# Deformable convolution of a four-stage network: a third offset buffer, a ring of three tents, and a rearranged start and end

## The chip, the core and the metric

The kernel runs on one core of one Trainium2 chip. Its engines work side by side and meet through semaphores: TensorE (PE, matmuls), VectorE (DVE), ScalarE (ACT), GpSimd (POOL) and SyncE (SP); the last two issue most of the DMAs. The metric is the device time of the core in microseconds, as a median of several runs.

## What is computed

The input is x of 8 images, 16 channels and 64 x 64 pixels, all in float32. Four stages follow one another: a gated scan over both axes (L0), an inverted-bottleneck convolution with mixed experts (L1), two deformable convolutions (L2), and two "distance" convolutions (L3). The change lies in L2, of which this is the core:

```python
def deform_conv(x, w, b, ow, ob):
    off = conv2d(x, ow, ob).reshape(Bn, K, 2, Hh, Ww)
    cy = iy + dy + off[:, :, 0]
    cx = ix + dx + off[:, :, 1]
    y0, x0 = jnp.floor(cy), jnp.floor(cx)
    wy, wx = cy - y0, cx - x0
    samp = gather(y0i, x0i, (1 - wy) * (1 - wx)) + gather(y0i, x0i + 1, (1 - wy) * wx) \
         + gather(y0i + 1, x0i, wy * (1 - wx)) + gather(y0i + 1, x0i + 1, wy * wx)
    return jnp.einsum('bckhw,ock->bohw', samp, w.reshape(w.shape[0], Cin, K)) + b

h = relu(group_norm1(deform_conv(x, w1, b1, ow1, ob1), g1, be1)) + x
h = relu(group_norm1(deform_conv(h, w2, b2, ow2, ob2), g2, be2)) + h
```

For each of K = 9 taps a convolution gives two offsets, the input is sampled bilinearly there, and the samples are contracted with the weights. A group norm over each image follows.

## The kernel before

The program is written engine by engine in one order that never changes: each engine runs its list and waits for semaphores. The two deformable layers are the loop over `L` (0 and 1).

**Offsets.** TensorE computes the offsets of 64 rows in four chunks of 16 rows (`convolve(m)`, L1269, 288 matmuls each). ScalarE copies a chunk out of PSUM (`copy_offsets`, L1049), VectorE bounds it (`bound_offsets`, L704 and L706) and takes the largest magnitude of each row (`reach`, L711; at the last chunk also L716). SyncE stores it to DRAM (`store_offsets`, L449). The raw offsets stand in two halves of `YA`, the bounded ones in two buffers at `D1`. A second rearrangement, DRAM to DRAM, makes one contiguous record of every batch of four rows (`arrange_batch`, L466, also SyncE). Between these TensorE turns the image (`turn_columns`, L1281), and GpSimd stores the turned columns (`store_columns`, L1457).

**Batches.** A layer has `NB` = 16 batches of four image rows, and a batch `NU` = 3 units of column blocks. For batch n GpSimd loads its record, spread over the partitions, in four DMAs of 576 KB (`load_batch`, L1484). It may do so when the record is arranged and the buffer is free: there are two buffers of offsets, so load n waits until the tent products of batch n-2 are ready. ScalarE takes the distances (`distances`, L1056), and for each unit two y terms (`y_terms`, L1067 and L1068). VectorE finishes the x tent of a batch (L723) and multiplies three tents for every unit (L729, L730, L731; nine operations a batch). The products go into a ring of `RING` = 4 slots. TensorE samples with them (`sample`, L1302 and L1307 at the image's edge, 48 or more matmuls a unit), and ScalarE copies the samples from PSUM (`copy_samples`, L1078). ScalarE then writes the y terms for the unit that is `RING` further on. After unit 0 of every second batch TensorE contracts the 18 sampled pieces of the eight rows before (`contract`, L1325 and L1330, 72 matmuls); ScalarE copies the result (`copy_rows`, L1093), and VectorE adds the rows that two contractions share (`add_shared_rows`, L750).

**Windows.** The image columns that a batch samples come from DRAM in four chunks of about 16 rows into two buffers (`load_windows`, L1471, GpSimd), and VectorE spreads the rows of a batch into a ring (`spread_windows`, L416), after unit 0 of the batch.

**Start.** All four offset convolutions precede the first sample on TensorE. ScalarE copies the fourth chunk between the y terms of units 2 and 3, and VectorE bounds it after batch 0.

**End.** When all rows are copied, VectorE counts the taps that reach beyond the bounded window (`far_samples`, from L860), whose table SyncE fetches once batch 14's tents are ready. For these inputs the count is zero and the branch over `far_block` is taken. Then come the statistics of the group norm (`channel_stats`, L534, eight chunks) and the normalisation.

## Time and profile before

| what | us |
|---|---|
| median of 3 runs (911.18 to 913.99) | 912.49 |
| the profiled execution, whole | 907.34 |
| its span in the profile | 905.5 |
| layer 0: tents of batch 0 finished, of batch 15 finished | 302.8, 498.5 |
| layer 1: tents of batch 0 finished, of batch 15 finished | 590.5, 785.4 |
| busy in the span: PE, DVE, ACT, POOL | 652.5, 592.2, 462.5, 124.3 |

All times inside the kernel are counted from the start of the span. The span is that of the core's instructions; the whole execution is 1.8 us longer. The two deformable layers take from about 241 to 814 us, so nearly two thirds of the kernel. A line such as "POOL arena L1484 <- DVE arena L731" says that an engine's instruction of line 1484 stood until one of line 731 on another engine had finished; `arena` is the one large on-chip buffer, and nearly every tile lies in it.

### The profile page before, as it was taken

The page shows a single profiled execution, that of the slowest core. Times are in us where ns is not written, and L with a number is a line of the kernel's source. Part 1 is how long each engine was busy: PE and PEld are TensorE (multiplying, and loading weights), DVE is VectorE, ACT ScalarE, POOL GpSimd, SP SyncE. Part 2 cuts the span into 40 slices and gives each one's busy share as a digit, 9 for nine tenths or more (in the row PEclk, how much of TensorE's full clock was granted, in tenths as well). Part 3 has the DMA queues.
Part 4 walks back from the last instruction along what each step waited for, and adds up shares of the span by engine and source line. Part 5 has one row for each costly group of instructions (what it writes and reads, how often), then busy time and mean ns, then how long its engine had stood idle before and what let it go on. Part 6 is the DMA issues. An engine that isn't in the chain of part 4 may idle for free.

```text
span 905.5 us, 30232 instructions
## 1 busy us (share of the span) xinstructions
PE 652.5 (72%) x13944; PEld 452.1 (50%) x13944; DVE 592.2 (65%) x823; ACT 462.5 (51%) x623; POOL 124.3 (14%) x187
## 2 busy tenths in 40 slices
PE   2409999999987486877787388567776876809493
PEld 1104555567854365655565255346655655605252
DVE  6894062211336978888887444798888888577365
ACT  3505424432332767768776141577777668532423
POOL 6000000000033113122210004222122111000000
PEclk9758999999999889898899779979999898958796
DMA  4000000000058866476543008956667555000002
GB/s 155 0 0 2 2 3 3 3 16 4 17 156 264 292 221 205 182 250 206 183 173 127 1 3 200 344 191 226 240 225 233 174 185 205 10 2 3 1 4 94
DMA packets 27754, 108.73 MB, mean 120 GB/s; under 512 B 10100, under 2 KB 14836, under 8 KB 23528
## 3 DMA queue, kind: packets, MB, share of 16 engines
q0 software_dynamic: 13376, 86.80, 28.5%
q1 hardware_dynamic: 14248, 19.97, 6.9%
q8 instruction: 110, 1.80, 0.8%
q14 instruction: 20, 0.16, 0.1%
HBM read 91.84 MB, written 19.65 MB: 123 GB/s over the span
## 4 chain that ended last, share of the span: by engine, by line
DVE 30%; PE 28%; DMA 21%; ACT 8%; issue 7%; POOL 3%; SPq 2%; DVEq 0%; ACTq 0%; POOLq 0%
DMA arena<-offsets_by_batch 17%; PE psum L1222 13%; DVE arena L730 5%; DVE arena L731 5%; PE psum L1198 5%; DVE arena L729 4%; POOL arena L1484 3%; PE psum L1414 3%; DVE arena L416 2%; PE psum L1269 2%; DMA offsets<-arena 2%; ACT arena L1068 2%; SPq L466 1%; PE psum L1235 1%; ACT arena L1067 1%
## 5 line engine op out<-in xcount | busy, mean ns | idle before, releaser
L1302 PE MATMUL psum<-arena 64*64 64x297 f32 (+4 forms) x4512 | 244.1, 367 | 111.0 <-ACT arena L1078 58.3
L1302 PEld LDWEIGHTS psum<-arena 64*64 64x64 f32 x4512 | 186.6, 146 | 167.7 <-issue 102.1
L1056 ACT ACTIVATE arena<-arena 128x2304 f32<-128x2304 f32 (+1 forms) x32 | 71.7, 2242 | 121.3 <-DMA arena<-offsets_by_batch 121.3
L1484 POOL DMA_DIRECT2D arena<-offsets_by_batch x128 | 77.7, 620 | 286.2 <-DVE arena L731 271.7
L1222 PE MATMUL psum<-arena 32*32 32x512 f32 x3456 | 115.1, 597 | 0.3 <-DVE arena L653 0.3
L1269 PE MATMUL psum<-arena 32*32 32x512 f32 x2304 | 83.1, 616 | 21.3 <-issue 15.5
L729 DVE SCALAR_TENSOR_TENSOR arena<-arena 128x792 f32<-128x792 f32 (+3 forms) x96 | 92.4, 963 | 7.8 <-ACT arena L1068 7.4
L1222 PEld LDWEIGHTS psum<-arena 32*32 32x32 f32 x3456 | 73.6, 103 | 39.9 <-issue 13.0
L730 DVE SCALAR_TENSOR_TENSOR arena<-arena 128x792 f32<-128x792 f32 (+3 forms) x96 | 92.2, 960 | 0.0
L731 DVE SCALAR_TENSOR_TENSOR arena<-arena 128x792 f32<-128x792 f32 (+3 forms) x96 | 92.2, 960 | 0.0
L1078 ACT ACTIVATE arena<-psum 128x792 f32<-128x792 f32 (+1 forms) x96 | 82.5, 860 | 9.0 <-PE psum L1307 8.2
L1068 ACT ACTIVATE arena<-arena 128x792 f32<-128x792 f32 (+3 forms) x96 | 84.9, 884 | 0.0
L1067 ACT ACTIVATE arena<-arena 128x792 f32<-128x792 f32 (+3 forms) x96 | 84.5, 881 | 0.0
L723 DVE TENSOR_SCALAR arena<-arena 128x2304 f32<-128x2304 f32 (+1 forms) x32 | 43.8, 1370 | 53.0 <-ACT arena L1056 53.0
L1012 ACT ACTIVATE arena<-psum,arena 128x512 f32<-128x512 f32 x48 | 29.8, 686 | 92.1 <-PE psum L1222 92.1
L1269 PEld LDWEIGHTS psum<-arena 32*32 32x32 f32 x2304 | 48.3, 104 | 53.0 <-issue 38.4
L1198 PE MATMUL psum<-arena 128*128 128x512 f32 x96 | 45.1, 618 | 36.7 <-DVE arena L628 36.7
L1325 PE MATMUL psum<-arena 64*64 64x256 f32 x1152 | 69.2, 384 | 2.0 <-ACT arena L1082 2.0
L643 DVE TENSOR_SCALAR arena<-arena 128x2048 f32<-128x2048 f32 x12 | 14.7, 1233 | 84.8 <-ACT arena L1012 84.8
L1325 PEld LDWEIGHTS psum<-arena 64*64 64x64 f32 x1152 | 49.5, 133 | 13.2 <-ACT arena L1082 2.2
L1003 ACT ACTIVATE arena<-psum,arena 128x512 f32<-128x512 f32 x48 | 36.0, 782 | 39.3 <-PE psum L1198 37.5
L1414 PE MATMUL psum<-arena 32*32 32x512 f32 x1152 | 44.5, 659 | 12.3 <-DVE arena L884 10.8
(137 smaller groups left out, 621.1 us busy)
## 6 DMA issues: line engine op xcount, KB each, us to landing
arena<-offsets_by_batch POOLq DMA_DIRECT2D x112, 576.0 KB, 8.1
arena<-offsets_by_batch POOLq DMA_DIRECT2D x16, 624.0 KB, 7.4
offsets<-arena SPq DMA_DIRECT2D x32, 256.0 KB, 10.7
offsets_by_batch<-offsets SPq DMA_DIRECT2D x184, 24.0 KB
columns<-arena POOLq DMA_DIRECT2D x8, 320.0 KB, 6.7
arena<-columns POOLq DMA_DIRECT2D x8, 320.0 KB, 11.3
arena<-in_x SPq DMA_DIRECT2D x4, 512.0 KB, 5.3
out<-arena SPq DMA_DIRECT2D x8, 256.0 KB, 2.2
```

What stands on the lines that cost most here:

```text
L729: v.scalar_tensor_tensor(term(0), term(0), 0.0, part(tx), ALU.min, ALU.mult)
L730: v.scalar_tensor_tensor(term(1), term(1), 1.0, part(tx), ALU.subtract, ALU.mult)
L731: v.scalar_tensor_tensor(term(2), part(ty), 0.0, part(tx), ALU.min, ALU.mult).then_inc(s_g, 1)
L1067: a.activation(term(0), part, ACT.Copy, scale=-1.0)
L1068: a.activation(term(1), part, ACT.Abs).then_inc(s_nd, 1)
L1078: ins = a.activation(ap(SAMP + n // 2 % 2 * SPAR + n % 2 * SLOTS * K * SX + u * WB[0], [[SR, 2], [SX, KR], [1, w]]), ap_ps(bank, [[CH, 2], ...
L1198: t_.matmul(ps(ch % 4, 0, CH), cols(W_HID + t * P, P), cols(XIN + ch * CH, CH), start=True, stop=True).then_inc(s_c1, 1)
L1222: ins = t_.matmul(ps_q(j, dw_bank(t, half) + i), cols(W_DIAG + (t * K + k) * Q, Q, Q * i, Q), ap(T_PAD[t % 4] + row * PW + k % 3, [[PW, CR ...
L1269: ins = t_.matmul(ps_q(2 * axis + h, conv_bank(m) + i), cols(W_CONV[L] + (axis * K + t) * Q, Q, Q * i, Q), ap(XA + (BLK * m + 8 * h + t // ...
L1302: ins = t_.matmul(ps_t(s, bank + r, first * K * w, many * K * w), window, ap(g_at(unit, d0) + first * TW + s * w, [[GS + TW, many], [SLOTS ...
L1325: ins = t_.matmul(ps_t(r, bank, (2 - k // 3) * SX, GR * SX), weights_, ap(SAMP + j % 2 * SPAR + r * SR + k * SX, [[K * SX, GR], [1, SX]], ...
L1484: g.dma_start(cols(in_at(n, 0), 2 * in_rows(n) * W, 64 * r + 32 * half, 32), bass.AP(batch_d.tensor, 2 * (4 * r * NB + n) * INS, [[0, QW / ...
```

## The change

It has five parts.

- **Three offset buffers.** Load n waits for the tents of batch n-3 instead of n-2. The room comes from moving the padded image `XA` and from `RING` = 3 instead of 4.
- **Ring of three.** ScalarE writes the y terms for the unit three further on.
- **Window chunks of eight rows.** Eight chunks a layer instead of four, the first of nine rows, the next of eight; the second no longer waits for the rest of the turned columns.
- **Fourth offset convolution.** TensorE does it after batch 0's three units, into other PSUM banks; ScalarE copies it after unit 2; VectorE takes its reach and bounds after batch 1 instead of batch 0, and the bounded result goes into the raw buffer's free half. SyncE stores it after arranging batch 4.
- **Far count and statistics.** The count comes directly after the last tents, and each chunk's statistics as soon as its rows are complete; the table is fetched one batch earlier.

The diff, cut to its core:

```diff
-CHUNKS = [(0, 17), (17, 33), (33, 49), (49, 64)]
-CHUNK_ROWS = 17
+NCHUNK = NB // 2
+CHUNKS = [(8 * c + 1 if c else 0, min(8 * c + 9, H)) for c in range(NCHUNK)]
+CHUNK_ROWS = 9
...
-        RING = 4
+        RING = 3
...
+        IN_AT = (IN, IN + 2 * INS, IN + 2 * INS + INK)
...
+        XA = YA + N
...
+        def bounded_at(m):
+            return RAW + NATS if m == 3 else D1 + m % 2 * NATS
...
         def conv_bank(m):
-            return 4 if m % 2 == 0 else 0
+            return 0 if m == 1 else 4
...
         def in_at(n, axis):
-            return IN + n % 2 * 2 * INS + axis * in_rows(n) * W
+            return IN_AT[n % 3] + axis * in_rows(n) * W
...
                 arrange_batch(L, 3)
+                arrange_batch(L, 4)
                 store_offsets(L, 3)
-                arrange_batch(L, 4)
                 sp.wait_ge(s_am, L + 1)
...
-                sp.wait_ge(s_g, UNITS * L + NU * (NB - 1))
+                sp.wait_ge(s_g, UNITS * L + NU * (NB - 2))
...
             def bound_offsets(L, m):
                 dve.wait_ge(s_cve, 16 * L + 4 * m + 4)
-                if m >= 2:
-                    dve.wait_ge(s_ds[m - 2], 64 * (L + 1))
+                if m == 2:
+                    dve.wait_ge(s_ds[0], 64 * (L + 1))
+                if m == 3:
+                    dve.wait_ge(s_red, 4 * L + 4)
...
                     batch(L, n)
-                    if n == 0:
-                        bound_offsets(L, 3)
+                    if n == 1:
                         reach(L, 3)
+                        bound_offsets(L, 3)
...
-                add_shared_rows(L, NM - 2)
-                add_shared_rows(L, NM - 1)
+                many = far_taps(L)
+                dve.wait_ge(s_yd, (NM - 1) * L + NM - 3)
+                for ch in range(NM - 3):
+                    chunk_stats(YA, ch)
+                for j in (NM - 2, NM - 1):
+                    add_shared_rows(L, j)
+                    dve.wait_ge(s_yd, (NM - 1) * L + j)
+                    chunk_stats(YA, j - 1)
                 dve.wait_ge(s_yc, NM * (L + 1))
-                far_samples(L)
-                channel_stats(YA, [s_yc] * 4, NM * (L + 1), vec(f"db{L}"))
+                link(chunk_stats(YA, NM - 1))
+                far_samples(L, many)
+                channel_stats(vec(f"db{L}"))
...
-                for unit in range(RING - 1):
+                for unit in range(RING):
                     y_terms(L, unit)
-                copy_offsets(L, 3)
-                y_terms(L, RING - 1)
...
                     copy_samples(L, unit)
                     if unit + RING < UNITS:
                         y_terms(L, unit + RING)
+                    if unit == NU - 1:
+                        copy_offsets(L, 3)
...
-                convolve(3)
-                pe.wait_ge(s_cve, 16 * (L + 1))
                 pe.wait_ge(s_ws, 16)
                 for unit in range(UNITS):
+                    if unit == NU:
+                        pe.wait_ge(s_cve, 16 * L + 12)
+                        convolve(3)
                     sample(unit)
...
-                if n >= 2:
-                    pool.wait_ge(s_g, UNITS * L + NU * (n - 1))
+                if n >= 3:
+                    pool.wait_ge(s_g, UNITS * L + NU * (n - 2))
...
-                    if n in (4, 8):
-                        load_windows(L, n // 4 + 1)
+                    if n >= 4 and n % 2 == 0:
+                        load_windows(L, n // 2)
```

`far_taps` is the first part of the old `far_samples` (the count and its load into a register), and `chunk_stats` one `bn_stats` of 512 columns.

**TensorE at the start of a layer, before.** L1269 is the offset convolution, L1281 the turning, L1302 and L1307 the first unit's samples:

```order
L1269 MATMUL psum<-arena 32x512 x144
L1281 MATMUL psum<-arena 64x128 x64
L1269 MATMUL psum<-arena 32x512 x432
L1302 MATMUL psum<-arena 64x198
L1307 MATMUL psum<-arena 64x33
```

**TensorE there, changed**, first the convolutions (L1300) and the first sample, then the end of unit 2's samples (L1333) and what follows:

```order
L1300 MATMUL psum<-arena 32x512 x144
L1312 MATMUL psum<-arena 64x128 x64
L1300 MATMUL psum<-arena 32x512 x288
L1333 MATMUL psum<-arena 64x198
L1338 MATMUL psum<-arena 64x33
...
L1333 MATMUL psum<-arena 64x180 x4
L1333 MATMUL psum<-arena 64x90 x4
L1300 MATMUL psum<-arena 32x512 x144
L1333 MATMUL psum<-arena 64x99 x4
L1333 MATMUL psum<-arena 64x198 x4
```

A quarter of the convolutions has moved from before unit 0 to between units 2 and 3.

**VectorE behind batch 0, before.** L731 ends batch 0, L416 spreads the windows of batch 1:

```order
L731 SCALAR_TENSOR_TENSOR arena<-arena 128x39x20
L704 TENSOR_SCALAR arena<-arena 128x2048 [waits bounded_offsets_stored_1,offsets_written]
L706 TENSOR_TENSOR arena<-arena 64x2048 [waits vector_chain]
L711 TENSOR_REDUCE arena<-arena 128x32
L716 TENSOR_REDUCE arena<-arena 128x8 [waits chunk_reach_ready]
L416 TENSOR_SCALAR arena<-arena 128x6x4x16 [waits samples_ready,even_windows_loaded]
```

**VectorE behind batch 1, changed.** L746 ends batch 1, L738 begins batch 2:

```order
L746 SCALAR_TENSOR_TENSOR arena<-arena 128x36x20
L726 TENSOR_REDUCE arena<-arena 128x32 [waits offsets_written]
L731 TENSOR_REDUCE arena<-arena 128x8 [waits chunk_reach_ready]
L718 TENSOR_SCALAR arena<-arena 128x2048 [waits chunk_reach_ready,offsets_written]
L720 TENSOR_TENSOR arena<-arena 64x2048 [waits vector_chain]
L738 TENSOR_SCALAR arena<-arena 128x2304 [waits offset_distances_ready]
```

The fourth chunk's four operations now stand a batch later, with the reach first.

**GpSimd's loads, changed**, from batch 1 to the windows of batches 4 and 5 (L1516 loads a batch with four DMAs, of which the first stands here; L1503 loads windows):

```order
L1516 DMA arena<-offsets_by_batch 32x1x4608 [waits offsets_arranged_1_of_four]
...
L1516 DMA arena<-offsets_by_batch 32x1x4608 [waits offsets_arranged_2_of_four]
...
L1516 DMA arena<-offsets_by_batch 32x1x4608 [waits tent_products_ready,offsets_arranged_3_of_four]
...
L1516 DMA arena<-offsets_by_batch 32x1x4608 [waits tent_products_ready,offsets_arranged_0_of_four]
...
L1503 DMA arena<-columns 64x5x128 [waits window_rows_spread,other_columns_stored,first_columns_stored]
```

Before, the load of batch 2 waited for tents too; the list is otherwise the same up to here.

## Rows read from the trace of the kernel before

**Rows 1.** Waits, whole run: who waited for whom, us in total, times, longest

```profile
POOL arena L1484 <- DVE arena L731: 271.7, 28, 19.5
...
ACT arena L1056 <- DMA arena<-offsets_by_batch: 121.3, 27, 8.7
```

**Rows 2.** Chain that ended last, inside layer 0: start us, us, what

```profile
446.56 2.54 POOL arena L1484 x3
449.10 9.26 DMA arena<-offsets_by_batch
```

**Rows 3.** Windows, batches 3 to 15: us, busy (x), clock, DMA share, GB/s

```profile
330.20:498.50 168.30, 127.75 (x2417) 99.19 (x2409) 139.90 (x203) 124.00 (x161) 36.28 (x56) 0.92 0.56 192
...
617.80:785.40 167.60, 124.98 (x2384) 98.94 (x2376) 139.62 (x203) 123.42 (x161) 32.07 (x56) 0.94 0.56 189
```

**Rows 4.** Groups of DVE, batches 3 to 15: busy, mean | idle before

```profile
L729 DVE SCALAR_TENSOR_TENSOR arena<-arena 128x792 f32<-128x792 f32 (+3 forms) x39 | 37.4, 960 | 4.0 <-ACT arena L1068 3.9
...
L723 DVE TENSOR_SCALAR arena<-arena 128x2304 f32<-128x2304 f32 (+1 forms) x13 | 17.8, 1368 | 24.5 <-ACT arena L1056 24.5
```

**Rows 5.** Timeline, DVE, one batch: start us, us, operation, [idle before <-releaser]

```profile
319.55 1.35 DVE L723 TENSOR_SCALAR arena<-arena 128x2304 f32<-128x2304 f32 x1
...
329.26 0.90 DVE L731 SCALAR_TENSOR_TENSOR arena<-arena 128x720 f32<-128x720 f32 x1
```

**Rows 6.** Timeline, ACT: distances, y terms, copies

```profile
441.02 0.78 ACT L1093 ACTIVATE arena<-psum 128x176 f32<-128x176 f32 x4
...
444.87 2.22 ACT L1056 ACTIVATE arena<-arena 128x2304 f32<-128x2304 f32 x1 [2.41 <-DMA arena<-offsets_by_batch]
447.00 0.92 ACT L1067 ACTIVATE arena<-arena 128x792 f32<-128x792 f32 x1
...
448.66 0.88 ACT L1078 ACTIVATE arena<-psum 128x792 f32<-128x792 f32 x1
449.42 0.85 ACT L1067 ACTIVATE arena<-arena 128x792 f32<-128x792 f32 x1
```

**Rows 7.** Timeline, PE: one unit of samples, one contraction

```profile
466.60 2.35 PE L1302 MATMUL psum<-arena 64*64 64x99 f32 x48 [1.12 <-DVE arena L416]
...
479.27 4.17 PE L1325 MATMUL psum<-arena 64*64 64x256 f32 x72
```

**Rows 8.** Windows, PE just after an idle stretch: us, PE busy, granted clock

```profile
449.60:453.00 3.40, 3.32 (x40) 0.50 0.89 293
```

**Rows 9.** Timeline, PE and ACT, offset convolutions of layer 0

```profile
241.30 9.42 PE L1269 MATMUL psum<-arena 32*32 32x512 f32 x276
...
268.69 2.42 ACT L1049 ACTIVATE arena<-psum,arena 128x512 f32<-128x512 f32 x4 [11.03 <-PE psum L1269]
281.82 2.42 ACT L1049 ACTIVATE arena<-psum,arena 128x512 f32<-128x512 f32 x4 [10.71 <-PE psum L1269]
```

**Rows 10.** Timeline, DVE, behind batch 0: fourth chunk, then windows

```profile
302.82 1.34 DVE L704 TENSOR_SCALAR arena<-arena 128x2048 f32<-128x2048 f32 x1
...
309.02 1.40 DVE L416 TENSOR_SCALAR arena<-arena 128x384 f32<-128x384 f32 x4
```

**Rows 11.** Timeline, DVE and ACT, end of layer 0

```profile
497.53 0.97 DVE L731 SCALAR_TENSOR_TENSOR arena<-arena 128x780 f32<-128x780 f32 x1
...
507.66 0.93 DVE L860 TENSOR_REDUCE arena<-arena 1x72 f32<-1x144 f32 x4
...
512.98 4.85 DVE L534 BATCH_NORM_STATS2 arena<-arena 128x6 f32<-128x512 f32 x8 [1.53 <-issue]
...
506.50 0.73 ACT L1093 ACTIVATE arena<-psum 128x154 f32<-128x154 f32 x4 [4.72 <-PE psum L1330]
```

**Rows 12.** DMA to landing: stores L449, then batch loads L1484

```profile
DMA to landing us min/median/max: 2.6/10.7/17.4
...
DMA to landing us min/median/max: 5.0/8.0/17.1
```

**Rows 13.** Timeline, DVE, first batch of layer 1

```profile
580.16 1.46 DVE L723 TENSOR_SCALAR arena<-arena 128x2496 f32<-128x2496 f32 x1 [3.19 <-ACT arena L1056]
```

More of the change, by code:

```diff
@@ L274, in build @@
         s_ds = [sem(f"bounded_offsets_stored_{m}") for m in range(4)]
-        s_in = [sem("even_offsets_loaded"), sem("odd_offsets_loaded")]
+        s_in = [sem(f"offsets_loaded_{i}_of_three") for i in range(3)]
         s_ar = [sem(f"offsets_arranged_{i}_of_four") for i in range(4)]
@@ L527, in link, with chunk_stats, channel_stats @@
                 dve.wait_ge(s_v, count[0])
-            def channel_stats(src, arrived, count_, shift=None):
-                for ch in range(NCH):
-                    if ch % 2 == 0:
-                        dve.wait_ge(arrived[ch // 2], count_)
-                    ins = v.bn_stats(cols(STAT + 6 * ch, 6), cols(src + ch * CH, CH))
-                link(ins)
+            def chunk_stats(src, ch):
+                return v.bn_stats(cols(STAT + 6 * ch, 6), cols(src + ch * CH, CH))
+            def channel_stats(shift=None):
                 link(v.bn_aggr(cols(MV, 2), cols(STAT, 6 * NCH)))
@@ L556, in norm_coefficients @@
                 v.tensor_tensor(cols(NC_ + 1, 1), beta, cols(NC_ + 3, 1), ALU.subtract).then_inc(s_coef, 1)
-            channel_stats(XIN, s_x, 16)
+            for ch in range(NCH):
+                if ch % 2 == 0:
+                    dve.wait_ge(s_x[ch // 2], 16)
+                ins = chunk_stats(XIN, ch)
+            link(ins)
+            channel_stats()
             dve.wait_ge(s_const, 16)
@@ L848, in far_block, with far_taps @@
                 own = ap(YA + blk * W, [[BLK * W, BR], [1, W]])
-                far_link(v.tensor_tensor(own, own, ap_ps(1, [[W, BR], [1, W]]),
-                                         ALU.add), last=True)
-            def far_samples(L):
+                far_link(v.tensor_tensor(own, own, ap_ps(1, [[W, BR], [1, W]]), ALU.add))
+                for ch in range(NCH):
+                    ins = chunk_stats(YA, ch)
+                far_link(ins, last=True)
+            def far_taps(L):
                 dve.wait_ge(s_fb, 32 * (L + 1))
@@ L874, in far_samples @@
                 dve.wait_ge(s_any, L + 1)
[L875 removed]
+                return loaded(dve, COUNT, 0, K * BLK)
+            def far_samples(L, many):
                 with dve.If(many > 0):
@@ L1111, in _ @@
                     if unit == 2 * NU:
-                        for m in range(4):
+                        for m in range(3):
                             act.wait_ge(s_ds[m], 64 * (L + 1))
+                        act.wait_ge(s_red, 4 * L + 3)
+                    if unit == 4 * 2 * NU:
+                        act.wait_ge(s_ds[3], 64 * (L + 1))
                         act.wait_ge(s_red, 4 * (L + 1))
```

37 lines of the change are left out of this document (19 added, 18 removed).

## Prediction

> **What bounds the kernel now.** I read the waits first, then the chain that ended last, then windows over the deformable stage, and last the timelines of its start and end. The waits [rows 1] show that GpSimd spends 271.7 us waiting until VectorE has finished a batch's tents, and that ScalarE then waits 121.3 us for the loads that GpSimd issues. The chain [rows 2] shows one turn: the issue takes some 2.5 us, the transfer another 9.3. Two buffers are the cause: load n may start only when the tents of batch n-2 are finished, so one buffer's turn is load, distances, tents, and two batches share it.
>
> The reader should see in the windows [rows 3] that batches 3 to 15 take 168.3 and 167.6 us in the two layers, 12.9 us a batch, while VectorE, the busiest engine, works 139.9 and 139.6 of them. What it lacks are 28.4 and 28.0 us, and in layer 0 the groups [rows 4] put 24.5 on the wait for the distances and 4.0 on the wait for the first y terms behind them. VectorE unhindered needs 10.6 us for a plain batch (319.55 to 330.16) [rows 5], and 139.9 / 13 = 10.76 with all that belongs to these batches.
>
> **Part B, the third buffer.** Load n now waits for batch n-3. In a turn of 10.8 us a load is issued at the end of batch n-3 and ScalarE wants it about 1.7 batches later, near 18 us. Issue 2.5 plus 9.3 to 10 us of transfer [rows 2] is some 12.5 us, and the median batch load lands in 8.0 us [rows 12]. So the load leaves the chain. Bandwidth allows it: the DMA share was 0.56 at 12.9 us a batch [rows 3], which is 0.67 at 10.8. The smaller window chunks have the same bytes in twice the packets, and their issues go from two to six inside the loop, some 2.5 us of GpSimd each, as for a load [rows 2], beside an engine that idles 9 us a batch; I cost them at nothing, and with a late load behind them at 2.5 us.
>
> What is late next? With three tent slots instead of four, ScalarE may write the terms of unit u+3 only after TensorE has sampled unit u. I followed two batches from the moment at which the tents of unit 0 of an even batch are ready. TensorE: sample 2.35, contraction 4.17, next sample 2.35 [rows 7], 8.9 us. ScalarE from there: copy 0.76, two y terms 1.5, rows 0.62, copy 0.76, y terms 1.5, copy 0.76, distances 2.13, y terms 1.66 [rows 6] (differences of starts, since the rows overlap), 9.7 us. VectorE's next unit: three operations at 0.9 us, 2.7 (the ninth of a batch is in [rows 5]). Sum 21.3 us for two batches, against VectorE's own 2 x 10.76 = 21.5. VectorE stays the bound with 0.2 us in hand, so every small stall of TensorE shows. I take 0.4 us of waits a batch, 5 us a layer; the ends are 0 and 16 (a turn of 12.0). Part B is -28.4 - 28.0 + 2 x 5 = **-46.4 us**.
>
> **Part A, the fourth offset convolution behind batch 0.** Before, TensorE did it while the first load was under way. Now it stands between the samples of batches 0 and 1. Batch 0's tents are finished at 302.8 [rows 10]; nothing ahead of them moves. Sampling unit 2 ends at about 305.3. A convolution takes between 9.4 us (276 of 288 matmuls in one piece) and 13.1 us (from one set of ScalarE's copies to the next, 268.69 to 281.82, with stalls); the one that ends at 268.69 took about 11.0 [rows 9], and I take that: 316.3. ScalarE has queued behind it, in order, the copy of the fourth chunk and then every copy of samples; it is done about 2 us later, 318.3. VectorE has batch 1's tents ready at about 313.6 (1.3 for windows, 10.5 for the batch, ScalarE's terms in time) and waits 4.7 us. Then come reach and bounds of the fourth chunk, 309.02 - 302.82 = 6.2 us [rows 10], to 324.5, and batch 2, 10.6, to 335.1. Before it ended at 330.16. Part A costs 5 us a layer, 3.4 to 7.1 by the two ends: **+10 us**.
>
> **Part C, the end of the layer.** Before, the last tents end at T = 498.5; VectorE idles until ScalarE has copied the last rows at T + 8.7 (506.50 + 0.73), then works on the far count, 3.8 us, loads the count and branches, 1.53, and takes eight chunk statistics, 4.85, to T + 19.3 [rows 11]. Now the far count begins at T: 3.8, load of the count about 0.5, five statistics at 0.61 make 3.0, shared rows 0.5 and a statistic 0.6, which is T + 8.4. The last rows arrive at T + 8.7: 0.5 for adding, two statistics 1.2, branch about 1: T + 11.4. That is 7.9 us less. How the 1.53 us divide is not shown; with all of them behind the statistics the gain is 7.3, with none 8.9. I take 7.5: **-15 us**. The flag that the count needs is fetched one batch earlier, so it is no wait.
>
> **Part D, the start.** The first window chunk has 9 rows instead of 17, so it stands less in the way of the first arrangement and load. Layer 0's VectorE is busy until then. In layer 1 it waits 3.2 us for the first distances [rows 13]: gain 0 to 3.2, I take **-1.5 us**.
>
> **Sum.** 10 - 46.4 - 15 - 1.5 = -52.9 us. The profiled execution took 907.34 us (span 905.5), which gives 854.4; the median of the runs shown is 5.15 us higher, and 912.5 - 52.9 = **859.6 us**. The bounds of the unknown costs: no waits, short convolutions, the best ends of C and D give about 842; 16 us of waits in each layer give 882 and, with convolutions of 13.1, 886.
>
> **Rivals.** First, **a unit at half clock**. After an idle stretch the granted clock was 0.50, that is 1.2 of 2.4 GHz, and 40 matmuls took 3.4 us [rows 8], 4.1 for a unit of 48 instead of 2.35. If that befalls one unit of the TensorE chain in each pair, the pair is 1.7 us longer, 0.85 a batch, 26 x 0.85 = 22: 882. For it: 0.2 us in hand. Against: idle stretches shrink from 4 us to below 2, and the mean clock is 0.92 to 0.94 already.
>
> Second, **SyncE's queue**. The store of the fourth chunk is now issued at 324.5 instead of 306.5, and the arrangement of batch 5 stands behind it on SyncE and in its DMA queue. Landing takes 2.6, 10.7, 17.4 us (least, median, most) for such stores [rows 12]. With 2 of issue, the median store, 4 for the arrangement (no row; the ends are those of the stores), 2.5 of issue and an 8.0 load, batch 5 is there at 351.7; it is wanted at 335.1 + 21.5 - 2.2 = 354.4. With a store of 17.4 it is 4 us late, with a slow load as well 13. I price it at 6 a layer: 872. The rule that speaks for it is in the Trainium skill, DMA: Bandwidth & Descriptors, Queues, rings and completion order: each DMA engine goes round the queues that have work, a packet at a time, so a long load takes turns with the stores. The trace agrees in that stores range from 2.6 to 17.4 us; by that rule load 2, which now starts at once, makes the second chunk's store late as well, and if both went by the longest rows the sum would be -41 instead of -52.9.
>
> Third, **the loads do not run ahead**: some gate that I read as open (arrangement, windows) holds each at the old turn. Then B is nothing: 10 - 15 - 1.5 = -6.5, 906. Against it: arrangement n waits only for the distances of batch n-4.
>
> Fourth, on the other side, **TensorE at half clock throughout the ring of three**. Samples of 4.1 and a contraction of 8.3 make the chain 16.5 + 9.7 + 2.7 = 29 us a pair, 14.5 a batch, 1.6 more than now: +41 + 10 - 15 - 1.5 = +34.5, 947 us. It turns the result to slower from a turn of 12.9 + 6.5 / 26 = 13.2 us, which takes six pairs in ten in that state. The granted clock over the stretch [rows 3] speaks against it, since TensorE will idle less, not more. The Trainium skill, TensorE: Matmul & The Clock Gate, Part 1, has activity as what releases the clock; by that the change raises it.
>
> **Chances.** Forecast, 850 to 868: 0.56. Below it, 842 to 850: 0.06. SyncE's queue, to 876: 0.13. A unit at half clock, to 886: 0.13. Between, to 905: 0.01. No running ahead, 906: 0.04. Within 0.3% of 912.5, which is about what a measurement of this kernel can tell from no change: 0.03. Slower: 0.04. Faster by over 0.3% is thus 0.93. The range 842 to 886 holds 0.88.
>
> **What the profile after would show.** Right: GpSimd's wait for VectorE is still long, but ScalarE's wait for the batch loads is nearly gone; batches 3 to 15 take 140 to 150 us with VectorE over 93% busy; VectorE waits about 5 us once, before the fourth chunk's reach; the convolution stands behind the samples of batch 0; the statistics end 11 to 12 us after the last tents. Wrong: ScalarE or TensorE stand between VectorE's units in each batch (ring), the first distances after batch 4 come late (SyncE), or the loads still start a batch before use. The prediction fails most if the stretch of 13 batches is over 155 us.

## Result and the profile after

The changed kernel takes **887.65 us** (median of 4 runs, 883.42 to 892.0) against 911.88 for the kernel before on the same chip: ratio 0.9731, 95% interval 0.9665 to 0.9797. The direction was right, the size was not: 859.6 was forecast with a range of 842 to 886. The profiled execution took 883.77 us (span 881.9, against 907.34 and 905.5), 23.6 less where 52.9 was expected.

The waits over the whole run show what the change did and what it put in place of the old wait.

```profile
POOL arena L1516 <- DVE arena L746: 177.5, 22, 15.5
...
ACT arena L1106 <- PE psum L1333: 92.2, 31, 7.1
...
PE psum L1333 <- DVE arena L425: 53.4, 13, 5.8
...
DVE arena L738 <- ACT arena L1084: 30.2, 29, 2.3
DVE arena L744 <- ACT arena L1096: 13.8, 34, 0.9
ACT arena L1084 <- DMA arena<-offsets_by_batch: 13.0, 2, 7.7
```

The wait for batch loads has gone from 121.3 us in 27 places [rows 1] to 13.0 in 2, those ahead of each layer's first batch. TensorE's wait (L1333, a sample) for VectorE's L425, the spreading of windows, has grown. It is 53.4 us in 13 places, and in the kernel before it was:

```profile
PE psum L1302 <- DVE arena L416: 22.1, 16, 2.1
```

The prediction priced this wait nowhere.

Windows of the changed kernel: batches 1 and 2 of layer 0, its batches 3 to 15, its end, then batches 3 to 15 of layer 1. Columns as in [rows 3].

```profile
302.88:334.95 32.07, 24.93 (x566) 17.35 (x561) 27.33 (x33) 20.65 (x27) 6.77 (x12) 0.91 0.75 266
334.95:494.70 159.75, 126.45 (x2444) 95.78 (x2436) 140.56 (x204) 123.75 (x161) 45.37 (x64) 0.93 0.58 191
494.70:506.10 11.40, 6.86 (x144) 5.41 (x144) 9.43 (x32) 3.85 (x9) 0.00 (x0) 1.00 0.00 1
606.91:767.65 160.74, 127.52 (x2428) 97.41 (x2419) 140.88 (x203) 123.42 (x161) 44.75 (x64) 0.93 0.57 189
```

Batches 3 to 15 took 168.3 and 167.6 us before [rows 3] and take 159.75 and 160.74 now, for the same work of VectorE. The forecast had about 145: VectorE's work and 5 us of waits. VectorE is now idle for 19.2 and 19.9 us of these stretches. That is 8.6 and 6.9 us saved where 23.4 and 23.0 were expected, and it is nearly the whole miss.

One pair of batches, VectorE first (start, duration, operation, idle time before it and its releaser):

```profile
373.91 1.36 DVE L738 TENSOR_SCALAR arena<-arena 128x2304 f32<-128x2304 f32 x1 [0.28 <-ACT arena L1084]
...
378.35 1.43 DVE L425 TENSOR_SCALAR arena<-arena 128x384 f32<-128x384 f32 x4
...
386.85 1.36 DVE L738 TENSOR_SCALAR arena<-arena 128x2304 f32<-128x2304 f32 x1 [1.54 <-ACT arena L1084]
388.60 0.99 DVE L744 SCALAR_TENSOR_TENSOR arena<-arena 128x792 f32<-128x792 f32 x1 [0.39 <-ACT arena L1096]
...
391.29 1.41 DVE L425 TENSOR_SCALAR arena<-arena 128x384 f32<-128x384 f32 x4
...
398.17 1.36 DVE L738 TENSOR_SCALAR arena<-arena 128x2304 f32<-128x2304 f32 x1 [0.34 <-ACT arena L1084]
```

TensorE over the same pair, then ScalarE:

```profile
379.88 3.94 PE L1333 MATMUL psum<-arena 64*64 64x99 f32 x48 [3.92 <-DVE arena L425]
383.54 4.26 PE L1356 MATMUL psum<-arena 64*64 64x256 f32 x72
387.58 4.38 PE L1333 MATMUL psum<-arena 64*64 64x99 f32 x96
392.79 2.35 PE L1333 MATMUL psum<-arena 64*64 64x99 f32 x48 [0.83 <-issue]
```

```profile
383.88 0.83 ACT L1106 ACTIVATE arena<-psum 128x792 f32<-128x792 f32 x1 [3.90 <-PE psum L1333]
384.60 2.21 ACT L1084 ACTIVATE arena<-arena 128x2304 f32<-128x2304 f32 x1
386.71 0.94 ACT L1095 ACTIVATE arena<-arena 128x792 f32<-128x792 f32 x1
387.54 0.95 ACT L1096 ACTIVATE arena<-arena 128x792 f32<-128x792 f32 x1
...
394.33 0.85 ACT L1096 ACTIVATE arena<-arena 128x720 f32<-128x720 f32 x1
395.20 0.83 ACT L1106 ACTIVATE arena<-psum 128x792 f32<-128x792 f32 x1
```

Read it as a loop. VectorE finishes the tents of unit 0 at 378.4. The samples of unit 0 need the windows of their batch too, and those are spread by L425 behind these tents, to 379.8. TensorE, idle for 3.92 us, samples for 3.94 us instead of 2.35. ScalarE copies the samples, takes the distances and the y terms of the next batch's unit 0, which has the same slot in a ring of three, since a batch has three units. Then VectorE makes the next tents of unit 0, from 388.60. So the turn is 12.94 us (373.91 to 386.85). The next one, with the sample in 2.35 us, is 11.32 (386.85 to 398.17). The pair takes 24.3 us, again and again to the end of the layer, where VectorE needs 21.5.

The other chain, through the contraction, is just as late. ScalarE's copy at 395.20 needs the second turn's sample, which ends at 395.14. It also stands behind ScalarE's own work, which ends at 395.18, and that work began when the sample behind the contraction was done. So two chains give the same 24.3 us here, and this trace alone does not say which one binds.

The granted clock in the two samples (window, length in us, PE busy, clock, DMA share, GB/s):

```profile
379.90:383.00 3.10, 3.10 (x40) 0.56 1.04 396
392.80:395.10 2.30, 2.30 (x48) 1.00 0.94 382
```

The first ran near the lower of TensorE's two levels (0.5, which is 1.2 GHz), the second at 2.4 GHz.

The end of layer 0, VectorE (T, the end of the last tents, is 494.70; compare [rows 11]):

```profile
494.70 0.93 DVE L878 TENSOR_REDUCE arena<-arena 1x72 f32<-1x144 f32 x4
...
499.44 3.07 DVE L539 BATCH_NORM_STATS2 arena<-arena 128x6 f32<-128x512 f32 x5 [0.94 <-DVE arena L891]
...
504.18 1.29 DVE L539 BATCH_NORM_STATS2 arena<-arena 128x6 f32<-128x512 f32 x2
506.10 0.37 DVE L543 BATCH_NORM_AGGREGATE arena<-arena 128x2 f32<-128x48 f32 x1 [0.63 <-DVE arena L539]
```

### The profile page after: what moved, and what is told of

Read it like the earlier page. It is cut to its first block, busy times and chain, and to the rows that moved or that the text cites. A ratio compares the mean times of both kernels' runs of the same rounds, so it can differ in the third digit from the quotient of the medians.

```text
span 881.9 us, 30272 instructions
## 1 busy us (share of the span) xinstructions
PE 653.4 (74%) x13944; PEld 450.6 (51%) x13944; DVE 595.5 (68%) x823; ACT 464.3 (53%) x623; POOL 158.9 (18%) x219
## 4 chain that ended last, share of the span: by engine, by line
PE 48%; DVE 20%; ACT 18%; DMA 6%; issue 5%; SPq 2%; POOL 0%; DVEq 0%; ACTq 0%
PE psum L1253 13%; PE psum L1333 12%; PE psum L1356 7%; PE psum L1229 5%; PE psum L1300 4%; ACT arena L1084 4%; ACT arena L1095 4%; PE psum L1446 3%; ACT arena L1096 3%; DMA arena<-offsets_by_batch 2%; DVE arena L745 2%; DVE arena L746 2%; DVE arena L425 2%; ACT arena L1106 2%; DMA offsets<-arena 2%
## 5 line engine op out<-in xcount | busy, mean ns | idle before, releaser
L1333 PE MATMUL psum<-arena 64*64 64x297 f32 (+4 forms) x4512 | 242.7, 365 | 111.2 <-DVE arena L425 53.4
L1333 PEld LDWEIGHTS psum<-arena 64*64 64x64 f32 x4512 | 182.2, 144 | 171.7 <-issue 121.9
L1516 POOL DMA_DIRECT2D arena<-offsets_by_batch x128 | 90.8, 721 | 247.6 <-DVE arena L746 177.5
L1253 PE MATMUL psum<-arena 32*32 32x512 f32 x3456 | 115.1, 597 | 0.3 <-DVE arena L665 0.3
L746 DVE SCALAR_TENSOR_TENSOR arena<-arena 128x792 f32<-128x792 f32 (+3 forms) x96 | 92.0, 959 | 0.0
L1300 PE MATMUL psum<-arena 32*32 32x512 f32 x2304 | 81.5, 611 | 10.3 <-DVE arena L945 5.8
L1096 ACT ACTIVATE arena<-arena 128x792 f32<-128x792 f32 (+3 forms) x96 | 86.2, 898 | 0.0
L1095 ACT ACTIVATE arena<-arena 128x792 f32<-128x792 f32 (+3 forms) x96 | 86.0, 895 | 0.0
L1356 PE MATMUL psum<-arena 64*64 64x256 f32 x1152 | 71.6, 391 | 2.5 <-ACT arena L1110 2.3
L1300 PEld LDWEIGHTS psum<-arena 32*32 32x32 f32 x2304 | 49.4, 104 | 37.7 <-issue 22.5
L1489 POOL DMA_DIRECT2D columns<-arena x16 | 9.9, 756 | 314.8 <-DVE arena L707 244.2
L738 DVE TENSOR_SCALAR arena<-arena 128x2304 f32<-128x2304 f32 (+1 forms) x32 | 44.0, 1375 | 30.2 <-ACT arena L1084 30.2
L1356 PEld LDWEIGHTS psum<-arena 64*64 64x64 f32 x1152 | 48.5, 137 | 16.6 <-ACT arena L1110 2.5
```

The lines of the kernel that those rows point to most:

```text
L746: v.scalar_tensor_tensor(term(2), part(ty), 0.0, part(tx), ALU.min, ALU.mult).then_inc(s_g, 1)
L1095: a.activation(term(0), part, ACT.Copy, scale=-1.0)
L1096: a.activation(term(1), part, ACT.Abs).then_inc(s_nd, 1)
L1253: ins = t_.matmul(ps_q(j, dw_bank(t, half) + i), cols(W_DIAG + (t * K + k) * Q, Q, Q * i, Q), ap(T_PAD[t % 4] + row * PW + k % 3, [[PW, CR ...
L1300: ins = t_.matmul(ps_q(2 * axis + h, conv_bank(m) + i), cols(W_CONV[L] + (axis * K + t) * Q, Q, Q * i, Q), ap(XA + (BLK * m + 8 * h + t // ...
L1333: ins = t_.matmul(ps_t(s, bank + r, first * K * w, many * K * w), window, ap(g_at(unit, d0) + first * TW + s * w, [[GS + TW, many], [SLOTS ...
```

## Experiments

There are three theories of what sets the longer turn. **S**: what lengthens the stretch is the loop of a tent slot, with two items that the prediction's chain did not have: 1.4 us for the windows, and 1.6 us of half clock in one sample of each pair. **C**: the chain is the prediction's own, through the contraction, without the windows and longer by the half clock alone. **L**: something in the loads still sets the turn. All ratios are to the kernel before on the same chip.

### The windows: early, and twice

```diff
                 for n in range(NB):
-                    if n < 2:
-                        spread_windows(L, n)
+                    spread_windows(L, n)
                     batch(L, n)
...
-                    if u == 0 and n >= 2:
-                        spread_windows(L, n)
```

> The changed kernel with one edit: VectorE spreads the window rows of a batch ahead of that batch's tents instead of behind the tents of its unit 0. Theory S (slot loop): with three tent slots unit 0 of a batch closes on unit 0 of the next: tents ready, windows spread 1.35 us (the sample of unit 0 waits for them), sample 2.35 (3.94 at half clock), copy 0.76, distances 2.1, y terms 1.7, tents 2.75; 11.3 and 12.95 us in turn, 24.3 for two batches. With the windows ahead the loop is 9.95 and 11.6 and VectorE (10.8) bounds at least every second batch: 21.5 to 22.4 us for two, 25 to 36 us less in all, 852 to 863 us. Theory C (the forecast's chain through the contraction, lengthened by half clock alone): the windows are not in it, 885 to 890 us. Theory L (loads still set the turn): 885 to 890 us.

Measured: **871.43 us** (869.89 to 871.55), ratio 0.9549 (0.9514 to 0.9585), 16.2 less than the changed kernel. TensorE's 13 waits for L425 are gone. So C and L, which expected nothing, are out as whole theories, but S's own number was missed as well, by 8 us. VectorE shows why; between 390.55 and 403.00 it waits in one place. Its timeline, then TensorE's:

```profile
379.62 1.35 DVE L738 TENSOR_SCALAR arena<-arena 128x2304 f32<-128x2304 f32 x1
...
390.55 1.35 DVE L738 TENSOR_SCALAR arena<-arena 128x2304 f32<-128x2304 f32 x1
...
396.34 0.98 DVE L744 SCALAR_TENSOR_TENSOR arena<-arena 128x792 f32<-128x792 f32 x1 [1.64 <-ACT arena L1093]
...
403.00 1.35 DVE L738 TENSOR_SCALAR arena<-arena 128x2304 f32<-128x2304 f32 x1
```

```profile
383.84 3.13 PE L1330 MATMUL psum<-arena 64*64 64x99 f32 x48 [3.13 <-DVE arena L746]
386.73 5.05 PE L1353 MATMUL psum<-arena 64*64 64x256 f32 x72
391.61 6.44 PE L1330 MATMUL psum<-arena 64*64 64x99 f32 x144
```

The turn 379.62 to 390.55 is 10.93 us, VectorE without a wait. The next is 12.45: the y terms of unit 1 come late, behind sample and contraction (both partly at half clock) and sample. That is the chain that the prediction followed; it comes to light once the windows are off both chains. Each theory was right about one chain.

One pair of this run shows what is left when the half clock stays away too. Behind the same idle stretch the sample at 407.22 took 2.35 us:

```profile
407.22 2.35 PE L1330 MATMUL psum<-arena 64*64 64x99 f32 x48 [3.12 <-DVE arena L746]
```

This pair (403.00 to 424.76) took 21.76 us, close to VectorE's own 21.5, where its neighbours took 23.4. Layer 1 has such a pair as well, with 2.35 us for the sample at 670.48 and 21.76 for the pair.

The other direction: the windows of batches 2 to 15 are spread twice, with the same values.

```diff
-                for a, b in parts:
-                    for i in range(4):
-                        ins = spread_part(v, c, a, b, i)
+                for again in range(2 if n >= 2 else 1):
+                    for a, b in parts:
+                        for i in range(4):
+                            ins = spread_part(v, c, a, b, i)
+                    if n >= 2 and not again:
+                        link(ins)
```

> The changed kernel with the window rows of batches 2 to 15 spread twice over, at the same place; the second time changes nothing in the result. Theory S: 1.4 us more in every turn, 14 batches in each of two layers, +38 us, 920 to 930 us. Theory C: VectorE has 12.1 us of work in a turn of 12.15, so nothing or up to 5 us, 885 to 893 us. Theory L: the same as C.

Measured: **934.23 us** (931.49 to 935.25), ratio 1.0247 (1.0209 to 1.0285): 46.6 more than the changed kernel, 1.7 for each of 28 batches, for an operation of 1.4 us. That is 4 us above S's range. The sample behind it now waits 5.45 us and takes 4.10:

```profile
391.81 4.10 PE L1336 MATMUL psum<-arena 64*64 64x99 f32 x48 [5.45 <-DVE arena L425]
```

A pair of turns is 27.3 us long, made of 14.5 and 12.8, so both turns lengthened, the one with the contraction and the one without. That fits the slot loop, which is in both, and not the contraction's chain, which meets L425 once in a pair and would give 1.4 us.

### The half clock

Forty matmuls on constants (80 records in the trace, which has two for each) stand ahead of unit 0 of each even batch from batch 4 on; they write columns 320 to 479 of the contraction's banks, which nothing reads, and TensorE would idle there.

```diff
+                    if unit % (2 * NU) == 0 and unit >= 4 * NU:
+                        keep_busy(unit // (2 * NU) - 1)
                     sample(unit)
```

> The changed kernel with 40 more matmuls, about 2 us, of constants into unused PSUM columns, ahead of the samples of unit 0 of every even batch from 4 on, where TensorE idles 3.9 us. They fill half of the idle stretch. Theory S: the sample behind them takes 2.35 instead of 3.94 us, 1.6 us less for two batches, six pairs in two layers, -19 us, 866 to 872 us. Theory C, in which half clock is the whole excess of 2.8 us over VectorE's 21.5: -34 us, 852 to 858 us. If an idle stretch of 3.9 us has nothing to do with the half clock: 886 to 892 us.

Measured: **872.72 us** (869.0 to 873.51), ratio 0.9555 (0.9515 to 0.9596). Here TensorE has 480 records more in a layer and the kernel is 14.9 us faster than the changed one. The unit before it, the filler and the unit behind it in TensorE's timeline, then the granted clock of the last (window, length, PE busy, clock, DMA share, GB/s):

```profile
374.41 4.73 PE L1333 MATMUL psum<-arena 64*64 64x99 f32 x96 [0.29 <-DVE arena L746]
378.96 2.90 PE L1375 MATMUL psum<-arena 64*64 64x160 f32 x80
383.14 2.35 PE L1333 MATMUL psum<-arena 64*64 64x99 f32 x48 [1.29 <-issue]
```

```profile
383.14:385.40 2.26, 2.26 (x52) 1.00 1.01 357
```

The pair 377.15 to 399.84 is 22.7 us, 1.6 less than 24.3. The number is just above S's range and far from C's 852 to 858. From the samples before it (to 379.14) to unit 0 (383.14) there are 4.0 us, as long as the idle stretch in the changed kernel. So the idle stretch is no consequence of the slow sample; a batch without a contraction gives TensorE some 7 us of samples in a turn of over 11. The Trainium skill, TensorE: Matmul & The Clock Gate, HAM oscillation, tells of a matmul kernel whose recurring DMA wait puts the engine back to half clock before every tile. The traces agree for a wait on other engines: the sample takes 3.94 us behind the recurring wait and 2.35 with the filler.

### The third buffer, and the ring of three, apart

The changed kernel, with each load waiting for batch n-2 again:

```diff
-                if n >= 3:
-                    pool.wait_ge(s_g, UNITS * L + NU * (n - 2))
+                if n >= 2:
+                    pool.wait_ge(s_g, UNITS * L + NU * (n - 1))
```

> The changed kernel with load n waiting for the tents of batch n-2 again, as with two offset buffers; everything else as changed. Theory S: the turn goes back to that of the loads, 12.9 instead of 12.15 us, 26 turns, +20 us, 903 to 912 us. Theory L (the loads set the turn either way): no more than +3 us, 885 to 891 us.

Measured: **916.9 us** (911.43 to 920.21), ratio 1.0055 (1.0025 to 1.0085). L falls: the third buffer's early loads are worth 29.2 us, even under the limit of the ring. S had 903 to 912 and was missed by 5 us, so its model of the loads is not complete. Without the early loads the rest of the change, gains at the end of the layer included, is half a percent slower than the kernel before.

The kernel before, with one tent slot less:

```diff
-        RING = 4
+        RING = 3
```

> The kernel before with one change alone: three tent slots instead of four, still two offset buffers. Theory S: the slot loop of three joins each batch's first unit to the windows of its own batch, and this costs even at a turn of 12.9 us, because the load and the loop take turns at being late. The changed kernel with two buffers took 916.9; adding back what its end of layer (15.7) and start (3.1) save and taking off the moved convolution (8.9) gives 926.8: expected 920 to 929. Theory L (the ring costs nothing as long as the loads set the turn, as the prediction supposed): 911 to 914.

Measured: **920.41 us** (914.38 to 926.38), ratio 1.0102 (1.0071 to 1.0132), 8.5 us slower. TensorE's wait for the windows has grown from 22.1 us to:

```profile
PE psum L1302 <- DVE arena L416: 65.6, 14, 6.3
```

So the slot that is missing makes this wait, with no other part of the change. The room for the third buffer was paid for with a tent slot, and with two buffers that slot has a price too. The prediction let it cost something only through the contraction.

And the kernel before, with the first experiment's edit alone:

> The kernel before, with its windows spread ahead of their batch's tents and nothing else. Control for theory S: with four tent slots and two offset buffers unit 0 does not close on the next batch's unit 0 and the loads set the turn, so the edit that was worth 16 us with three slots is worth nothing here: 908 to 915. If an earlier spreading is of use in itself (TensorE starts each batch sooner): 895 to 905. If it delays VectorE's tents and so the next load: 915 to 925.

Measured: **911.85 us** (902.86 to 913.42), ratio 0.9981 (0.9955 to 1.0008). No difference: with four slots and two buffers the windows are on no chain. ScalarE waits 118.2 us for loads, and VectorE waits for ScalarE's distances. The two rows of the waits:

```profile
ACT arena L1053 <- DMA arena<-offsets_by_batch: 118.2, 22, 8.4
...
DVE arena L723 <- ACT arena L1053: 53.0, 15, 5.0
```

The same two-line edit is worth nothing there and 16 us in the changed kernel, which ties its worth to the three slots and the early loads together. No run had four slots with early loads, so the share of each is not shown.

### The moved convolution

The fourth convolution is ahead of all samples again, its reach and bounds behind batch 0.

```diff
-                    if unit == NU:
-                        pe.wait_ge(s_cve, 16 * L + 12)
-                        convolve(3)
                     sample(unit)
```

> Undoes one part of the change: the fourth offset convolution stands ahead of all samples again, and its reach and bounds behind batch 0; three buffers, three tent slots and the new end of the layer stay. The trace of the changed kernel put this part's price at 4.8 us in layer 0 and 4.1 in layer 1. If it is a plain term of the sum, this kernel takes 875 to 880 us (887.65 less 8.9, from 883.8 for the profiled execution 874.9), and batches 3 to 15 take the 159 to 161 us that they take in the changed kernel. If the moved convolution pays for itself (the first batches start from the same moment and TensorE was idle anyway), no difference: 884 to 889. If its place also sets the phase in which the ring of three settles, the stretch of batches 3 to 15 itself changes by more than 2 us.

Measured: **885.21 us** (883.02 to 885.25), ratio 0.9707 (0.9671 to 0.9743): 2.4 less than the changed kernel, not 8.9. From the end of batch 0 to the start of batch 3 it takes 32.64 us (307.24 to 339.88) where the changed kernel takes 34.43 (302.88 to 337.31), and in layer 1 31.36 against 33.52; and layer 1's first distances come late by 4.02 us instead of 2.14. So 1.8 + 2.2 - 1.9 = 2.1 us. Part of what I had read as the convolution's cost is the ring's, since VectorE comes to a stop in batches 1 and 2 whether the convolution is there or not. Its row at the start of batch 2, with the convolution out of the way:

```profile
326.23 1.36 DVE L738 TENSOR_SCALAR arena<-arena 128x2304 f32<-128x2304 f32 x1 [2.19 <-ACT arena L1084]
```

How large that part is stays open. The changed kernel's four runs lie between 883 and 892, the two intervals overlap, and its wait ahead of the fourth chunk's reach is not steady. It was 3.30 and 2.79 us in the two layers of its own trace, and 6.80 and 6.09 in the trace of the experiment on the end of the layer, further down, whose code is the same up to there:

```profile
320.42 2.29 DVE L726 TENSOR_REDUCE arena<-arena 128x32 f32<-128x2048 f32 x1 [6.80 <-ACT arena L1075]
```

With both edits:

> Both edits: windows spread ahead of their batch's tents, and the fourth convolution ahead of all samples. The first alone took 871.43 us. If the terms add, 871.4 less 8.9: 860 to 865. If spreading the windows early had removed part of the wait behind the moved convolution already (VectorE would then be waiting for the fourth chunk with its windows done), the second edit is worth less than 5: 866 to 871.

Measured: **863.03 us** (862.23 to 866.21), ratio 0.9471 (0.9431 to 0.9512). Here the same move is worth 8.4 us (871.43 less 863.03; 7 by the two ratios, since the kernels ran on different chips), and the runs do not overlap. With the windows early VectorE waited 5.96 and 3.10 us for the moved convolution, and here it has no wait to put in their place but 0.87 us at batch 2.

### All together, and the contraction's place

> The two edits of the kernel before it in this list and 40 idle matmuls ahead of unit 0 of each even batch from batch 4 on, which keep TensorE from going into that unit at half clock. Theory S (slot loop and half clock): with windows first, even turns were 11.9 to 12.5 us where odd ones were 10.9; if the half clock is what still lengthens them, turns become 10.9 to 11.2 and the time is 12 turns of 0.5 to 0.8 us per layer less: 848 to 855. Theory C (the chain through the contraction is what is left, and it holds at full clock too): even turns stay at 11.5 or more, 857 to 863. If the extra matmuls stand in the way of the chain themselves: 864 or more.

Measured: **853.82 us** (844.73 to 856.86), ratio 0.9329 (0.9267 to 0.9392), within S's range. The filler for batch 2 as well:

```diff
-                    if unit % (2 * NU) == 0 and unit >= 4 * NU:
+                    if unit % (2 * NU) == 0 and unit >= 2 * NU:
```

> The kernel with all three edits (853.82), with the 40 idle matmuls ahead of unit 0 of batch 2 as well. In its trace that unit still took 3.93 us, and the contraction behind it made VectorE wait 1.3 us; the turns from batch 2 on took 11.6 and 12.5. Theory S with C: the two turns lose 1 to 2 us per layer: 849 to 853. If the first pair is slow for another reason (first copies, edge batch): no difference, 853 to 856.

Measured: **850.58 us** (846.05 to 855.94), ratio 0.9316 (0.9264 to 0.9369). The gain of 3 us is smaller than either kernel's spread, so this run alone decides nothing. And on top of that:

```diff
-                    if u == 0 and n % 2 == 0 and n >= 2:
+                    if u == 1 and n % 2 == 0 and n >= 2:
                         contract(n // 2 - 1)
...
-                    if u == 1 and n % 2 == 0 and n >= 2:
+                    if u == 2 and n % 2 == 0 and n >= 2:
                         copy_rows(L, n // 2 - 1)
```

> The kernel before it in this list, with the contraction of a pair behind unit 1 of the next batch instead of behind unit 0 (and ScalarE's copy of its rows one unit later). Theory C: with the slot loop out of the way the chain through the contraction is what lengthens some turns; behind unit 1 it no longer stands between unit 0, whose samples ScalarE needs before the distances, and unit 1: turns come nearer to 10.85 and the time falls by 1 to 6: 843 to 850. If the chain merely moves to unit 2, no difference. If VectorE is the bound already, no difference either; if it collides with the next batch's unit 0, 855 or more.

Measured: **846.98 us** (838.96 to 850.5), ratio 0.9296 (0.9273 to 0.9319), the fastest of all and 40.7 us below the changed kernel. Its profiled execution is the one of 838.96. Windows from the first operation of batch 3 to T, in both layers, first of the changed kernel, then of this one:

```profile
337.31:494.70 157.39, 124.09 (x2392) 93.72 (x2384) 140.51 (x203) 121.39 (x159) 43.69 (x61) 0.93 0.58 192
609.06:767.65 158.59, 125.58 (x2387) 95.98 (x2379) 140.80 (x202) 121.27 (x159) 44.75 (x64) 0.92 0.57 188
```

```profile
330.55:471.16 140.61, 131.04 (x2848) 103.97 (x2840) 137.96 (x199) 119.99 (x158) 48.19 (x64) 1.00 0.65 216
583.65:723.46 139.81, 131.36 (x2848) 100.61 (x2840) 137.87 (x199) 119.98 (x158) 49.28 (x64) 1.00 0.64 214
```

VectorE works 137.96 of 140.61 us, 10.8 us a batch. That is the bound to which the prediction had expected the change to come within 0.4 us. VectorE waits for no distances in these stretches, while in the kernel ahead of it some turns still took 12 us. That 3.6 us of medians separate the two is again within the spread.

### The end of the layer

```diff
-                many = far_taps(L)
-                dve.wait_ge(s_yd, (NM - 1) * L + NM - 3)
-                for ch in range(NM - 3):
-                    chunk_stats(YA, ch)
                 for j in (NM - 2, NM - 1):
                     add_shared_rows(L, j)
-                    dve.wait_ge(s_yd, (NM - 1) * L + j)
-                    chunk_stats(YA, j - 1)
                 dve.wait_ge(s_yc, NM * (L + 1))
-                link(chunk_stats(YA, NM - 1))
+                many = far_taps(L)
+                dve.wait_ge(s_yd, (NM - 1) * L + NM - 1)
+                for ch in range(NM):
+                    ins = chunk_stats(YA, ch)
+                link(ins)
```

> Undoes the new order at the end of the layer alone: VectorE adds both last shared rows and waits for ScalarE's last rows before it works on the far count and takes the eight chunk statistics; all else is as in the changed kernel. If the two traces read rightly (statistics end 11.4 us after the last tents instead of 19.3), this kernel is 2 x 7.9 = 15.8 us longer: 901 to 906. If the end's gain was made somewhere else (the earlier fetch of the flag, the order on SyncE), less than 8: under 896.

Measured: **905.6 us** (899.3 to 912.25), ratio 0.9941 (0.9905 to 0.9978): 18.0 more than the changed kernel, with a spread of 13 us. VectorE idles again, and the far count starts behind it:

```profile
505.74 0.48 DVE L765 TENSOR_TENSOR arena<-arena,psum 128x44 f32<-128x44 f32 x4 [8.48 <-ACT arena L1119]
506.14 0.93 DVE L878 TENSOR_REDUCE arena<-arena 1x72 f32<-1x144 f32 x4
```

So two thirds of what the whole change gained (15.7 of 23.6 us by the traces) is made at the end of the layers.

## Why the prediction was wrong, point by point

- **What bounds the kernel**: right. The loads had set the turn, and VectorE's 10.8 us is the bound below, which the last kernel above reaches.
- **Part B, the load leaves the chain**: right. ScalarE waits for no load behind the first batch, and undoing it costs 29.2 us.
- **Part B, what is late next**: wrong, and this step carries the miss. The step is "VectorE stays the bound with 0.2 us in hand". The chain was begun "from the moment at which the tents of unit 0 of an even batch are ready", as if the sample could start then. Two items were missing. First, the sample of unit 0 waits for the windows as well, and VectorE spreads them behind these tents: 1.4 us. The row for L416 stood in the trace of before with 1.40 us [rows 10], and TensorE's wait for it in [rows 7]; I used that row for the sample's 2.35 us and passed over the bracket behind it. With four slots and two buffers that wait cost nothing, as the kernel before with early windows shows; with three slots the next batch's unit 0 needs the sample. Second, the half clock, 3.94 instead of 2.35: 1.6 us. The prediction's own sum of 21.3 us for a pair, with these two, gives 21.3 + 1.4 + 1.6 = 24.3, which is what the trace shows. Apart from that chain, the prediction had no loop from one use of a slot to the next. That loop meets the windows in both turns, comes to the same 24.3 us, and is the one that spreading the windows twice lengthened.

The sum through the contraction for the kernels above, in us for a pair of batches in layer 0, from batch 4 on:

| kernel | windows | half clock | sum | read |
|---|---|---|---|---|
| changed | 1.4 | 1.6 | 24.3 | 24.3 |
| kept busy | 1.4 | 0 | 22.7 | 22.7 |
| windows first | 0 | 1.6, once 0 | 22.9, once VectorE's 21.5 | 23.4, once 21.8 |
| all three | 0 | 0 | 21.3, VectorE's 21.5 | 21.8 to 22.7 |

- **The size that followed**: I allowed 0.4 us of waits a batch, with 16 us a layer as the far end. The stretch of 13 batches has 14.9 and 16.1 us more than the 144.9 and 144.6 forecast. So B was -15.4 and not -46.4, 31.0 us short. The other terms, 1.2 less for A, 0.7 and 1.6 more gained in C and D, and 1.9 lost outside the parts (the last stage, not looked into), make that the 29.4 us by which the profiled execution missed 854.4. The allowance of 0.2 us "in hand" was a warning: where two chains are this close, each microsecond left out of a pair counts six or seven times a layer.
- **Part A**: forecast +10; by the same boundaries 32.07 - 27.34 = 4.7 in layer 0 and 4.1 in layer 1, so the sum was nearly met. The terms were off: the convolution took 9.89 us and not 11.0, and VectorE waited 3.30 and 2.79 us for it and not 4.7, and waits for ScalarE in batch 1 that the term left out (0.93 and 0.40 us in layer 0) filled most of the rest. Undoing this part gave 2.4 us in the changed kernel, within its spread, and 7 to 8.4 with the windows early. That the sum came out near +10 is in part luck.
- **Part C**: right. The aggregate starts at T + 11.40 and in layer 1 at T + 11.35, where 11.4 was forecast; 15.7 us in the traces, 18.0 by undoing it, 15 expected.
- **Part D**: -3.1 us in the trace, -1.5 forecast. It was not undone by itself. The same stretch, from the end of layer 0 to layer 1's first tents, is 62.3 us before, 59.2 here, and 58.9 to 61.8 in the five experiments whose code is the same in it, so the trace does not tell the two numbers apart.
- **The rivals**: the first, a unit at half clock, was right in place and size (1.7 us a pair forecast, 1.6 read), with a chance of 0.13. It is about half of the miss; the other half, the windows, was in no rival. The argument against it, that idle stretches shrink to below 2 us, failed. The idle stretch ahead of an even batch is 3.9 us, and still 3.1 with the windows early. SyncE's queue did not bind: ScalarE waited for no load there. The loads did run ahead. TensorE went to half clock in one sample of a pair, not throughout; the granted clock of the stretch stayed at 0.93.
- **What would show it wrong** named the ring and a stretch of over 155 us, and both came. The price for it went no further than 16 us a layer, and VectorE was idle for 19 to 20.

What stays open: the two-buffer kernel and the kernel before with three slots do not add up. The changed kernel with two buffers should be 18 us below the kernel before with three slots, less 2.4 for the convolution, and is 3.5 below. The four window issues more in GpSimd's queue, ahead of loads that are on the chain with two buffers, may account for it; that was not tried apart. In the two traces 5.9 us of the gap lie in batches 3 to 15 of both layers, 3.5 in the batches before, and 2.9 ahead of layer 0's first tents. The last is no effect of the edits: in the changed kernel and five experiments that are the same up to there, these tents begin anywhere from 292.0 to 297.3 us. The window chunks of eight rows were never undone by themselves, so what they cost or give is open too.

## What to carry to other kernels

When a ring loses a slot, write down every wait of each unit in it, also the waits that come from the order of another engine's list. Then close the loop from one use of a slot to the next; here a batch of three units in a ring of three tied each unit 0 to the next one. Compare that loop with the bound before pricing the gain, and where both are within a few tenths of a microsecond, price each omitted microsecond times its count. A wait that costs nothing in the kernel before (1.4 us of windows behind the tents) is worth moving at the same time as the change that makes it count.

## What the hardware showed that I had not expected

- More matmuls made the kernel faster: 40 of them ahead of one sample in each pair took 887.65 to 872.72 us. The sample behind the idle 3.9 us ran at a granted clock of 0.56, behind the filler at 1.00.
- The half clock came back in every pair. In the changed kernel the twelve samples behind an idle stretch of 3.9 to 4.0 us took 3.55 to 4.24 us instead of 2.35, and the turns alternate near 12.9 and 11.3 us from batch 5 to the end. The idle stretch ahead of the slow sample is there without the slow sample (4.0 us in the kernel with the filler). Behind an idle stretch of the same 3.12 us the samples of the kernel with early windows took anything from 2.35 to 3.94 us.
- Spreading the windows twice, 1.4 us more in each turn, lengthened a pair by 3.0.
- The same edit had different prices in different surroundings: moving the convolution back 2.4 or 8.4 us, spreading windows early 0 or 16.
